# Image stage of a three-stage kernel: how many of the 25 depthwise taps TensorE makes

## What is computed

```python
x = x + _dwconv(x, pos_w, pos_b)                    # 3 x 3 depthwise
y = _ln(xh, ln1_g, ln1_b)
qkv = y @ qkv_w + qkv_b
logits = jnp.einsum('bpc,bqc->bpq', q_win * SCALE, k_win)
_, idx = jax.lax.top_k(logits, TOPK)                # 4 windows for each of 49
att = jnp.einsum('bpqhd,bpkhd->bphqk', q_pix * SCALE, k_sel)
att = jax.nn.softmax(att, axis=-1)
o = jnp.einsum('bphqk,bpkhd->bpqhd', att, v_sel).reshape(B, P2, W2, C)
v_img = kv[..., QK:].transpose(0, 3, 1, 2)
lepe = _dwconv(v_img, lepe_w, lepe_b)               # 5 x 5 depthwise, the 25 taps
o = (o + lepe) @ wo_w + wo_b
xh = xh + o
z = _ln(xh, ln2_g, ln2_b)
z = jax.nn.gelu(z @ mlp_w1 + mlp_b1, approximate=False) @ mlp_w2 + mlp_b2
xh = xh + z
```

## Time and profile before

| | |
|---|---|
| median of 3 runs | 10605.33 us (10599.95 to 10654.83) |
| the profiled execution | 10650.4 us, span 10648.6 us |
| busy share of the span | TensorE 81%, VectorE 84%, ScalarE 59%, GpSimd 56% |
| mean granted clock of TensorE | 0.898 of full speed |

### The profile page before, as it was taken

How to read it: one execution, slowest core, us unless ns; L and a number is a source line. 1 busy time by engine, 2 the same in 40 slices (tenths; PEclk the granted TensorE clock), 3 DMA queues, 4 the chain that set the end, 5 groups by cost and what they waited for, 6 DMA issues and landing times. The chain is left out here.

```text
span 10648.6 us, 196346 instructions
## 1 busy us (share of the span) xinstructions
PE 8596.3 (81%) x61658; PEld 3647.3 (34%) x61658; DVE 8923.8 (84%) x10968; ACT 6268.9 (59%) x11797; POOL 6010.0 (56%) x3646
## 2 busy tenths in 40 slices
PE   6999999989999997787877777877877777777760
PEld 3555555555555553222222222222222222222210
DVE  7777777777777775999999999999999999999984
ACT  5666666666666664555555555555555555555543
POOL 3222222222222221878878878787778878778760
PEclk9999999999999998888888888898888888888875
DMA  2223322232332321111111111111111111111129
GB/s 67 68 68 75 73 68 68 72 78 74 74 75 73 76 73 39 37 33 37 37 33 37 37 33 38 36 33 39 34 33 39 35 33 41 33 35 39 33 49 266
DMA packets 855791, 591.00 MB, mean 56 GB/s; under 512 B 621424, under 2 KB 725872, under 8 KB 848464
## 3 DMA queue, kind: packets, MB, share of 16 engines
q1 hardware_dynamic: 751440, 423.61, 17.3%
q0 software_dynamic: 49152, 100.76, 2.6%
q10 hardware_dynamic: 54016, 51.91, 1.6%
HBM read 109.27 MB, written 103.81 MB: 20 GB/s over the span
## 5 line engine op out<-in xcount | busy, mean ns | idle before, releaser
L1190 POOL TENSOR_TENSOR b_hh<-b_hh,b_cn 128x1024 f32<-128x1024 f32 x1600 | 3834.4, 2414 | 1053.3 <-DVE b_hh L1445 1052.9
L1445 DVE TENSOR_TENSOR_SCAN b_hh<-b_dA,b_ub 128x512 f32<-128x512 f32 x3200 | 3865.7, 1208 | 0.0
L1314 ACT ACTIVATE b_dA<-b_db,b_negA 128x448 f32<-128x448 f32 x3200 | 1980.6, 634 | 1761.4 <-PE b_db L1539 1755.4
L278 POOL DMA_DIRECT2D kvsel<-kv x1536 | 1104.2, 721 | 2877.1 <-issue 2456.0
L1437 DVE TENSOR_TENSOR b_ub<-b_ub,b_bn 128x512 f32<-128x512 f32 x3200 | 2174.8, 680 | 378.2 <-PE b_ub L1539 358.3
L1539 PE MATMUL b_ub<-b_rows,b_pick 96*64 96x512 bf16 x6400 | 1405.1, 440 | 1008.2 <-DVE b_hh L1445 949.8
L1539 PEld LDWEIGHTS b_ub<-b_rows,b_pick 96*64 96x64 bf16 x6400 | 359.1, 110 | 3194.7 <-DVE b_hh L1445 2535.5
L1539 PE MATMUL b_db<-b_rows,b_pick 96*64 96x512 bf16 x6400 | 1267.2, 419 | 218.7 <-ACT b_dA L1314 214.7
L554 DVE SCALAR_TENSOR_TENSOR oacc<-vpad,vec,oacc 128x1064 f32<-128x1064 f32 (+1 forms) x934 | 1199.4, 1301 | 11.4
L1575 PE MATMUL b_acc<-b_hh,b_gather 64*32 64x512 f32 x12800 | 1050.7, 719 | 2.8 <-POOL b_hh L1190 2.8
L395 ACT ACTIVATE prob<-score,nmax 128x256 f32<-128x256 f32 (+1 forms) x1600 | 737.4, 479 | 161.0 <-issue 91.3
(11 more groups left out here) (185 smaller groups left out, 12247.5 us busy)
## 6 DMA issues: line engine op xcount, KB each, us to landing
b_rows<-b_term SPq DMA_DIRECT2D x2400, 64.0 KB, 2.0
kvsel<-kv SPq DMA_DIRECT2D x1600, 64.0 KB, 2.1
kvsel<-kv POOLq DMA_DIRECT2D x1536, 64.0 KB
xpad<-in_x SPq DMA_DIRECT2D x18, 1568.0 KB, 10.7
ys<-ysb ACTq DMA_DIRECT2D x16, 1600.0 KB, 9.4
b_yc<-ys SPq DMA_DIRECT2D x100, 256.0 KB, 2.7
xr<-b_xo SPq DMA_DIRECT2D x100, 256.0 KB, 2.7
x<-x3pad SPq DMA_DIRECT2D x16, 1568.0 KB, 18.2
```

The costliest lines, as they stand in the source:

```text
L278: eng.dma_start(kvsel[:, slot, j, :, WPIX * t:WPIX * (t + 1)].unsqueeze(1), kv[:, bass.ds(at[t], 1), :, :]).then_inc((s_kv, s_kg)[j][slot] ...
L1190: nc.gpsimd.tensor_tensor(out=now, in0=now, in1=cn[:, par, :].unsqueeze(1).broadcast_to([C, 2, HT]), op=ALU.mult).then_inc(s_pm, 1)
L1314: nc.scalar.activation(later(dA[:, k % DEEP, :]), later(db[k % 2][:, :]), ACT.Exp, scale=negA[:, 8 * q + e:8 * q + e + 1]).then_inc(s_a, 1)
L1445: nc.vector.tensor_tensor_scan(hh[:, k // 2 % PDEEP, HT * (k % 2):HT * (k % 2 + 1)], dA[:, k % DEEP, :], ub[(UNITS * par + k) % 3][:, :], ...
```

## The change

```diff
@@ -68,7 +68,7 @@
-        PTAP = 5
+        PTAP = 4
         VTAP = LEPE_TAPS - PTAP
         CUTS = (0, 19, 38, H)
         THIRDS = len(CUTS) - 1
         LEPES = VTAP * THIRDS
         SLOTTED, EARLY = {3: 5, 4: 5, 5: 5, 6: 2}, 25
         PACE = (LEPES - EARLY) / 24
```

## The result

The changed kernel took 10568.73 us (median of 18 runs, 10541.39 to 10601.41) where the kernel before took 10618.59 (18 runs). The ratio is 0.9953, with a 95% interval of 0.9943 to 0.9964: faster by 38 to 61 us, 50 in the middle. The forecast had been 25 us less than before, 10580. The change itself was forecast at half of its size.

A forecast was written before the change was run, and what follows sets the result against it. The prediction held that no single engine fills the attention loop; waits between TensorE, VectorE and ScalarE set its length. Step changes summed to -1.2, the tail made it -1.55 per image, -25 us over 16 images: 10605 to 10580, range 10520 to 10645.

The forecast's parts named there:

- the walk: Attention loop summed step by step, each from one L525 to the next, plus the tail: -1.55 us per image; chance 0.67.
- steps 1 to 5: Attention loop's start: second taps lengthen steps 1, 3 and 5, step 4 loses TensorE's double tap; together +1.0 us.
- 6 to 13: Attention loop: steps 8 and 12 become 4.42 by VectorE, -0.5; steps 9 and 13 stay; running sum +0.5 us.
- 14 to 17: Attention loop: 14, 15 and 17 stay; 16 goes from 4.05 to 3.65 without TensorE's double tap; running sum +0.1.
- 18 to 23: Attention loop: step 21 falls from 5.14 to 3.97, its merge now behind one tap; together -1.3 us.
- Behind the loop -0.35: TensorE's run into the projection: -0.21 from the last group's taps, perhaps 0.14 more from the last double tap.
- I take the dips as unchanged: TensorE's clock drops behind merge waits, 1.5 us each, 2.4 us per image, assumed to stay; without any, 38 us lower.
- the band of 0.96 to 0.98: Sign of being wrong: TensorE's granted clock over the attention loops moves away from 0.96 to 0.98.
- an image's period: Sign of being wrong: the time per image in the image stage falls by more than 3.3 us or rises.
- More dips: Rival, chance 0.08: TensorE's idle time in the loop grows, a dip behind each of five merges; +58 us, 10663.
- TensorE binds: Rival, chance 0.15: TensorE bounds the image stage and all 6.0 us per image are gained; -96 us, 10509.
- VectorE binds: Rival, chance 0.10: VectorE bounds the attention loop and each added tap costs its full 1.3 us; +57, 10662.

The follow-up runs named there:

- the fronts filled: Kernel before and changed kernel, each with filler matmuls in the merge waits and six more in the front's 2.9 us wait: 10558.70 and 10546.92 us.
- The filled kernel before: Kernel before plus four useless matmuls in TensorE's wait for L405 at each of steps 14, 18 and 22: 10580.84 us, ratio 0.9964.
- TensorE's half alone: Against the kernel before, TensorE makes four taps, VectorE keeps its 20, the 25th tap is left out: 10544.45 us, ratio 0.9923.
- VectorE's half alone: Against the kernel before, VectorE makes 21 taps in the changed order, TensorE still five: 10637.88 us, ratio 1.0010.
- 15 fillers: Even-step kernels with fillers before the loop's first (4) and second (11) scores, six in the front; against before, five taps 0.9900, four taps 0.9871.

## Why the prediction had the sign right and half of the size

- The loop is shared by three engines, and TensorE's 6.0 us come back in part: right. The shortest steps fell by 1.05 us per image, and the walk had -1.2: +1.3 for steps 1 to 5 (forecast +1.0), -0.8 for 6 to 13 (-0.5), -0.5 for 14 to 17 (-0.4), -1.1 for 18 to 23 (-1.3). Its single steps were 3.65, 4.42, 3.97 and 5.14; measured were 3.5, 4.4, 3.9 and 5.14 to 5.20. The one that it missed is step 20, 4.66 for 4.42, with L536 at 0.86 us in place of 0.62.
- Behind the loop -0.35 was expected. With the fronts filled -0.3 is measured. In the plain kernels it doesn't show: the stretch is 127.3 us on average before and 127.4 after, because the front's dip came in all sixteen images where it had come in thirteen.
- These two are -1.35 x 16 = -22 us, against -25 forecast.
- "I take the dips as unchanged" is the step that failed. It left out a term as large as the sum. Leaving out the low stretch at each loop's start, dips went from 25 to nine: at steps 14, 18 and 22 from 25 to three, and of six new ones five are at step 6, where a merge now follows two taps. Sixteen fewer at 1.5 us are 24 us, and with the -22 that is -46, for 50 measured. The two profiles split their 53 us so: 17 in the shortest steps, 29 in what steps 4 to 23 take beyond them, 8 in the same of the first four steps, and 1 longer behind the loop. The filled kernel before shows the price of a dip by itself; that their number changed is read from one profile of each kernel.
- Two of the prediction's own signs of being wrong spoke up. The loops' granted clock left the band of 0.96 to 0.98: seven loops read 1.00. And an image's period fell by 53.1 / 16 = 3.3 us, just at its bound.
- Why the dips went is only partly shown. The experiments show that the waits behind merges bring the dips (fill them and they are gone) and that none comes behind a merge where every merge follows one tap (waits of 0.8 to 1.1 us). Three waits of 2.00 us became one of 2.19 at step 14 and two of 1.70 and 1.77 at steps 18 and 6. But step 14, with a wait no shorter than before, has three dips in sixteen images where it had eleven, step 18 none and step 6 five. TensorE's half alone has three waits of 1.7 and eight dips at step 14, one at 18, none at 22; VectorE's half alone has three of 2.00 and eleven dips at step 6, two at 14, two at 18, and five at step 2. So the length of the wait alone doesn't say whether a dip comes; what else does stays open.
- More dips (10663): refuted, there were fewer. The rule of the Trainium skill (TensorE: Matmul & The Clock Gate, Part 4: PE-mode transpose), that transposes don't count for the clock gate as matmuls do, had pointed to more. The rule isn't refuted, since no run has transposes without matmuls.
- TensorE binds (10509, -96): refuted by the change's own -38 to -61, and by its half alone, of whose 6.0 us the shortest steps kept 2.7. VectorE binds (10662, +57): refuted by its half alone at +11 (-3 to +25).

## What to carry to other kernels

Where several engines share a loop, walk its steps in order of time: the place of an instruction (a merge behind two taps or behind one) was worth 96 us, twice what moving a tap to another engine was; somewhat over half of the 96 is shorter steps, the rest dips. And count the low-clock stretches behind TensorE's waits before and after as a term of the sum; a wait that costs nothing by itself can cost some 1.5 us of the work behind it (2.0 us waits here), and matmuls of no use in such a wait gave it back.

## What the runs showed of the hardware that was not expected

- Filling 2.0 us waits with useless matmuls made the kernel 38 us faster, with all the work the same. The clock's levels are 1.2 and 2.4 GHz, and in the profiles' records of it each of the 25 low stretches behind a 2.00 us wait begins within 1.4 us after its end.
- The low clock at the loop's start (10 to 14 us in most images) did not go away with 15 fillers: in most images a shorter one came some 6 to 12 us later, among the steps that it then slowed.
- In step 20 of the changed kernel VectorE's L536 takes 0.86 us for two in each image, and in step 14 0.80 in most; in nearly all other steps it is 0.61 to 0.67. What lengthens it was not tried.
